# Two cross-attentions over 77 keys on one Trainium2 core: dense queries with masked keys, row sums taken with the values, division in token order

## The reference, cut to what matters

```python
    def _L0_xattn_ref(x, y, q_w, q_b, kv_w, kv_b, qn_w, qn_b, kn_w, kn_b, out_w, out_b):
        q = (x @ q_w.T + q_b).reshape(b, s1, H, hd).transpose(0, 2, 1, 3)
        kv = (y @ kv_w.T + kv_b).reshape(b, s2, 2, H, hd).transpose(2, 0, 3, 1, 4)
        k, v = (kv[0], kv[1])
        q = _layernorm(q, qn_w, qn_b)
        k = _layernorm(k, kn_w, kn_b)
        q = _apply_rope(q) * scale
        attn = jnp.einsum('bhqd,bhkd->bhqk', q, k)
        attn = jax.nn.softmax(attn, axis=-1)
        o = jnp.einsum('bhqk,bhkd->bhqd', attn, v)
        o = o.transpose(0, 2, 1, 3).reshape(b, s1, c)
        return o @ out_w.T + out_b
    def _L1_xattn_ref(xq, xkv, Wq, Wkv, Wout, bout):
        q = (xq @ Wq.T).reshape(B, SQ, NUM_HEADS, HEAD_DIM)
        kv = (xkv @ Wkv.T).reshape(B, SKV, 2, NUM_HEADS, HEAD_DIM)
        k, v = (kv[:, :, 0], kv[:, :, 1])
        att = jax.nn.softmax(jnp.einsum('bxhd,byhd->bhxy', q, k) * scale, axis=-1)
        x = jnp.einsum('bhxy,byhd->bxhd', att, v).reshape(B, SQ, H)
        return x @ Wout.T + bout
```

## Time and profile before

| | |
|---|---|
| runs | 2087.87, 2095.12, 2100.6 us; median 2095.12 |
| the profiled execution | 2091.41 us; span 2089.7 us from its first to its last instruction |
| mean granted TensorE clock | 0.933 |
| busy share of the span | PE 86%, PEld 68%, DVE 56%, ACT 48%, POOL 36% |
| L0x | about 330 to 568 us of the span; its loop 367 to 552 |
| L1x | about 1337 to 1534 us; its loop 1366 to 1520 |

### The profile page before, as it was taken

One profiled execution on the slowest core, in us unless ns is written; L12 is line 12 of the kernel. 1 busy time (PEld: TensorE's weight loads), 2 busy tenths in 40 slices (PEclk: granted clock), 3 DMA queues, 4 the chain that ended last, 5 costly groups with the idle time before them and its releaser, 6 DMA issues. The chain is left out here.

```text
span 2089.7 us, 41893 instructions
## 1 busy us (share of the span) xinstructions
PE 1797.7 (86%) x15668; PEld 1421.4 (68%) x15668; DVE 1178.4 (56%) x3027; ACT 1003.5 (48%) x2376; POOL 745.4 (36%) x680
## 2 busy tenths in 40 slices
PE   6889875899659999769999999599959995999994
PEld 5767764676448888646777776476647774788883
DVE  3666664575454545435555555456548782457774
ACT  4655552354234545345554445244436662356663
POOL 2434342776314242323333333311124452334443
PEclk9999998998779999979999999799969997999997
DMA  2000002000054342530000000201010415723334
GB/s 67 12 12 22 12 12 74 1 22 22 26 211 129 114 142 61 147 113 2 11 12 12 11 12 6 71 2 32 16 54 17 134 37 173 262 84 54 52 52 101
DMA packets 97872, 125.52 MB, mean 60 GB/s; under 512 B 8555, under 2 KB 84795, under 8 KB 97643
## 3 DMA queue, kind: packets, MB, share of 16 engines
q1 hardware_dynamic: 84378, 105.07, 15.3%
q0 software_dynamic: 13296, 17.77, 4.9%
HBM read 85.02 MB, written 39.89 MB: 60 GB/s over the span
## 5 line engine op out<-in xcount | busy, mean ns | idle before, releaser
L1876 POOL TENSOR_TENSOR L1a_probs<-L1a_probs,L1a_rinv 128x1024 f32<-128x1024 f32 x64 | 121.2, 1894 | 270.0 <-DVE L1a_rinv L2191 270.0
L1873 POOL TENSOR_TENSOR L0a_probs<-L0a_probs,L0a_rinv 128x256 f32<-128x256 f32 (+1 forms) x128 | 103.1, 826 | 189.6 <-DVE L0a_rinv L2191 189.6
L2183 DVE CUSTOM_DVE_ANT_0 L1a_sbias<-L1a_psS,L1a_bias 128x256 f32<-128x256 f32 x256 | 93.3, 421 | 108.7 <-PE L1a_psS L1984 108.6
L2136 ACT ACTIVATE L1a_probs<-L1a_sbias,L1a_nmx 128x256 f32<-128x256 f32 x256 | 126.5, 497 | 47.5 <-DVE L1a_nmx L2183 47.4
L2863 POOL DMA_INDIRECT moe_sums<-moe_y,moe_xg x39 | 83.4, 2139 | 134.3 <-DVE moe_y L3162 122.4
L2136 ACT ACTIVATE L0a_probs<-L0a_sbias,L0a_nmx 128x128 f32<-128x128 f32 (+1 forms) x256 | 112.8, 443 | 28.8 <-DVE L0a_nmx L2183 28.8
L2447 POOL DMA_INDIRECT ec_sums<-ec_yk,ec_token_at x32 | 59.0, 1845 | 189.1 <-ACT ec_yk L2568 184.2
L2633 DVE TENSOR_TENSOR ec_h<-ec_sg,ec_psU 128x512 f32<-128x512 f32 x64 | 44.0, 687 | 118.7 <-ACT ec_sg L2555 118.7
L2941 PE MATMUL moe_psY<-moe_wts,moe_hT 128*128 (+1 forms) x440 | 104.0, 379 | 0.8 <-ACT moe_hT L3008 0.8
L2183 DVE CUSTOM_DVE_ANT_0 L0a_sbias<-L0a_psS,L0a_later 128x128 f32<-128x128 f32 (+1 forms) x256 | 76.2, 354 | 44.3 <-PE L0a_psS L1981 43.9
L2480 PE MATMUL ec_psG<-ec_xs,ec_wt 128*128 128x512 f32 x384 | 99.0, 394 | 2.1 <-issue 2.1
(11 more groups left out here) (533 smaller groups left out, 5061.8 us busy)
## 6 DMA issues: line engine op xcount, KB each, us to landing
shelf<-in_L_ffn_w_gate SPq DMA_DIRECT2D x8, 1024.0 KB, 9.1
shelf<-in_L_ffn_w_up SPq DMA_DIRECT2D x8, 1024.0 KB, 12.8
ec_wd<-in_L_ffn_w_down SPq DMA_DIRECT2D x8, 1024.0 KB, 6.1
moe_rows<-blank SPq DMA_DIRECT2D x1, 5070.0 KB, 19.1
moe_xg<-moe_rows SPq DMA_DIRECT2D x39, 130.0 KB, 2.1
moe_wts<-in_L_ffn_e_gate SPq DMA_DIRECT2D x8, 512.0 KB, 10.2
moe_wts<-in_L_ffn_e_up SPq DMA_DIRECT2D x8, 512.0 KB, 9.9
moe_wts<-in_L_ffn_e_down SPq DMA_DIRECT2D x8, 512.0 KB, 10.1
```

Of the source, the lines that this page charges most:

```text
L1873: last = pool.tensor_tensor(v, v, bcast(rinv[:, r, :, t], 2, KEYS[t]), ALU.mult)
L1876: last = pool.tensor_tensor(v, v, bcast(rinv[:, r, :, :].rearrange("p h t -> p (h t)"), 2, S), ALU.mult)
L2136: ins = act.activation(probs[:, r, j, at], sbias[:, g % 2, j, at], ACT.Exp, bias=nmx[:, r, j, t:t + 1], scale=-1.0, accum_out=sums[:, r, j ...
L2183: last = dve.tensor_tensor_reduce(out=sbias[:, g % 2, j, at], in0=psS[:, slot + j, at], in1=added, scale=-1.0, scalar=LARGE, op0=ALU.add, ...
```

## The change

It is confined to `context_stage`, so to L0x and L1x.

- **Dense queries, masked keys.** Queries are kept as two tiles of 128 rows a batch with eight heads each, without padding. Keys come in two copies, `keys[:, o, par]`, multiplied by the mask `keep`, so that of two neighbouring heads one is zero. A second copy `marked`, made by GpSimd in `mark_keys`, has a one in a row that the masked head leaves free. `shift` no longer adds in place: it writes `shifted`, queries times `others` plus the transposed maxima. The turned scores multiply `marked` by `shifted`.
- **Row sums with the values.** The two unused 16-column groups of `vs` are 1 instead of 0, so that one product gives values and row sums. `row_sums` and `ones` are gone. `values` of the two steps go to the two halves of `psO`.
- **Division in token order.** ACT copies `psO` (`copy_values`), TensorE transposes it (`turn_values`), DVE's `out_norm` takes reciprocals of 8 columns and multiplies into `oM`, TensorE transposes back (`turn_back`), ACT rounds from `psO`, and `out_low` is now on DVE.
- **Order.** The transposed maxima have a bank of their own (`psT`, `turn_top`), and `NF` is 2. `turn_top` stands behind the second turned block instead of ahead of it. On DVE `row_max(n+2, 0)` stands ahead of `shift(n+1)`, and `spread` behind it.
- **Fronts.** Weight preparation is one operation for a matrix instead of four or eight, the masks are made on DVE (`set_masks`, `set_columns`) instead of memsets on GpSimd, and two broadcast transfers replace eight small ones. The `keep_busy` matmuls of the loops are gone; three (L0x) or six (L1x) stand in the fronts, beside the six ahead of L0x's first query item.

The core of the diff:

```diff
-    NF = 3
+    NF = 2
...
             def row_max(n, pair):
                 dve.wait_ge(s_ready[pair], n + 1)
                 if n >= 2:
-                    dve.wait_ge(item_ready, ready(("top",), n - 2))
+                    dve.wait_ge(top_ready, n - 1)
...
             def shift(n):
                 b, st = divmod(n, NST)
-                dve.wait_ge(item_ready, ready(("top",), n))
-                q = qs[:, b % 2, st, :]
-                dve.tensor_tensor(q, bank(("top",), n)[:, 0:S], q, ALU.add).then_inc(q_shifted, 1)
+                dve.wait_ge(top_ready, n + 1)
+                if n >= 2:
+                    dve.wait_ge(k_ready, 2 * n - 2)
+                dve.scalar_tensor_tensor(out=shifted[:, n % 2, :], in0=qs[:, b % 2, st // 2, :],
+                                         scalar=others[:, st % 2:st % 2 + 1], in1=psT[:, 0:S],
+                                         op0=ALU.mult, op1=ALU.add).then_inc(q_shifted, 1)
...
             def out_norm(o):
-                dve.wait_ge(r_ready, 2 * o + 2)
-                dve.reciprocal(rinv[:, o % 2, :], psO[:, S:2 * S]).then_inc(r_inverse, 1)
-                dve.wait_ge(r_inverse, o + 1)
-                if o >= 2:
-                    dve.wait_ge(o_low, o - 1)
-                dve.tensor_tensor(oN[:, o % 2, :], psO[:, 0:S], rinv[:, o % 2, :], ALU.mult).then_inc(o_norm, 1)
+
+                dve.wait_ge(o_turned, o + 1)
+                if o:
+                    dve.wait_ge(o_back, o)
+                turned = [psO[:, r * S:(r + 1) * S].rearrange("p (t j e) -> p (t j) e", t=TT, j=4) for r in range(2)]
+                for r in range(2):
+                    dve.reciprocal(rinv[:, r, :], turned[r][:, :, HD * (1 - r)]).then_inc(r_inverse, 1)
+                dve.wait_ge(r_inverse, 2 * o + 2)
+                for r in range(2):
+                    last = dve.tensor_tensor(oM[:, :, r, :], turned[r][:, :, HD * r:HD * (r + 1)], bcast(rinv[:, r, :], 2, HD),
+                                             ALU.mult)
+                last.then_inc(o_norm, 1)
...
+            def mark_keys(what, b):
+
+                wait_taken(pool, what, b)
+                o, at = key_columns(what, b)
+                for par in range(2):
+                    last = pool.tensor_scalar(marked[:, o, par, at], keys[:, o, par, at], one[:, par:par + 1], None, ALU.add)
+                last.then_inc(k_marked, 1)
...
+            def turn_top(n):
+
+                pe.wait_ge(s_max[0], n + 1)
+                pe.wait_ge(s_max[1], n + 1)
+                for t in range(TT):
+                    last = pe.transpose(psT[:, t * P:(t + 1) * P], top[:, n % 2, t, :], ident[:])
+                last.then_inc(top_ready, 1)
+
+            def turn_values(o):
+
+                pe.wait_ge(o_copied, o + 1)
+                for r in range(2):
+                    for t in range(TT):
+                        at = slice(r * S + t * P, r * S + (t + 1) * P)
+                        last = pe.transpose(psO[:, at], oE[:, at], ident[:])
+                last.then_inc(o_turned, 1)
+
+            def turn_back(o):
+
+                pe.wait_ge(o_norm, o + 1)
+                for t in range(TT):
+                    last = pe.transpose(psO[:, S + t * P:S + (t + 1) * P],
+                                        oM[:, 4 * t:4 * t + 4, :, :].rearrange("p j r d -> p (j r d)"), ident[:])
+                last.then_inc(o_back, 1)
...
             for n in range(N):
-                st = n % NST
                 turned_beside_scores(n, 0)
                 for what, b in slot(n, 0):
                     item(what, b)
                 if n:
                     values(n - 1)
-                if n + 1 < N:
-                    item(("top",), n + 1, (1, 0, 2, 0)[st] if rope else (1, 1 if n >= 4 * NST else 0, 0, 0)[st])
+                if n % 2 == 1 and n >= 3:
+                    turn_back((n - 3) // 2)
                 turned_beside_scores(n, 1)
-                if n:
-                    row_sums(n - 1)
+                if n + 1 < N:
+                    turn_top(n + 1)
+                if n % 2 == 0 and n >= 2:
+                    turn_values(n // 2 - 1)
                 for what, b in slot(n, 1):
                     item(what, b)
...
+            def copy_values(o):
+
+                act.wait_ge(v_done, 2 * o + 2)
+                if o:
+                    act.wait_ge(o_turned, o)
+                act.activation(oE[:], psO[:], ACT.Copy).then_inc(o_copied, 1)
...
                 b, st = divmod(n, NST)
                 if n + 1 < N:
                     row_max(n + 1, 1)
-                if st == 0 and b >= 2:
-                    spread(b - 2)
                 if rope and n == 2:
                     scale_k(1)
                 for what, at in slot(n, 0):
                     take(what, at)
+                if n + 2 < N:
+                    row_max(n + 2, 0)
                 if n + 1 < N:
                     shift(n + 1)
-                if n + 2 < N:
-                    row_max(n + 2, 0)
-                if st % 2 == 0 and n >= 2:
+                if st == 0 and b >= 2:
+                    spread(b - 2)
+                if n % 2 == 0 and n >= 2:
                     out_norm(n // 2 - 1)
+                if n % 2 == 1 and n >= 3:
+                    out_low((n - 3) // 2)
```

More of the change, by code:

```diff
@@ L426, in _ @@
                 b, st = divmod(n, NST)
-                if st % 2 == 1 and n >= 3:
-                    out_low(n // 2 - 1)
                 if st == 0 and b >= 2:
@@ L434, in _ @@
                     place_q(pool, 1)
+                for what, at in slot(n - 1, 1) + slot(n, 0) if n else []:
+                    if what[0] == "kT":
+                        mark_keys(what, at)
                 if rope and b + 2 < B:
@@ L560, in item @@
                                              start=(c == 0), stop=(c == KD - 1))
-                elif what[0] == "top":
-                    pe.wait_ge(s_max[0], b + 1)
-                    pe.wait_ge(s_max[1], b + 1)
-                    for t in range(TT):
-                        last = pe.transpose(ps[:, t * P:(t + 1) * P], top[:, b % 2, t, :], ident[:])
                 else:
@@ L665, in _ @@
             values(N - 1)
-            row_sums(N - 1)
+            turn_values(N // 2 - 1)
+            turn_back(N // 2 - 1)
             item(("out", 0), B - 1)
@@ L1064, in _ @@
             out_norm(N // 2 - 1)
+            out_low(N // 2 - 1)
             set_off(B - 2)
```

319 lines of the change are left out of this document (158 added, 161 removed).

## The result

Over 20 runs the changed kernel took 2080.97 us in the median (2068.48 to 2086.93), the kernel before 2100.7 (2087.23 to 2108.95, also 20 runs). The ratio is 0.9904, with a 95% interval of 0.9888 to 0.9920: 1.0% or about 20 us faster. The change measured is −20, and the median 2080.97 lies within rival A's 2060 to 2084, 6 us above the forecast because the kernel before was slower in these runs too.

What follows compares the result with a forecast made beforehand. TensorE was taken to bound the kernel; saved work, waits, fronts and clock summed to −12 us in L1x and −6 in L0x, from a profiled 2091.4 to 2073, stated as 2075 us for the median. The range was 2042 to 2107.

Steps and rivals of the forecast that it cites:

- rival A: Whole kernel: half the saved work is given back in waits, 2060 to 2084 us; chance 0.42.
- The bound: Both loops: TensorE is the bound, so work taken from it counts; net work L0x −23.1, L1x −27.6 us.
- The new waits: Both loops: waits that the new order brings, +16 us in L1x and +14 in L0x.
- the shift: End of steps: TensorE waits for the longer chain of maxima and shift, +10 us in L1x, +4 in L0x.
- The shorter reciprocals: Both loops: small reciprocals replace long ones and remove waits of the values, −5 us in L1x, −4 in L0x.
- the spread: Step 0 of a batch: LayerNorm statistics ahead of out_norm delay the next values, +6 us in L1x, +4 in L0x.
- ScalarE, +3: L0x's loop: ScalarE finishes a normalised row in front of an exponential in six batches, +3 us.
- GpSimd's marks: L0x: mark_keys on GpSimd stands ahead of the inverse roots, +3 us, bounds 0 and 13.
- The fronts: Before the loops: weight preparation saves about 2 us in L1x, masks, columns and first marks add 2 in L0x; together 0.
- a sign of being wrong: Fronts of both stages: the prediction is wrong if they move by over 5 us.
- The clock: Both loops: one or two further stretches at 1.2 GHz, +5 us in L0x, +7 in L1x; bounds −10 and +60.
- rival C: TensorE falls to 1.2 GHz in whole batches, clock under 0.85 in either loop, about 2117 us; chance 0.20.

Runs made afterwards that it cites:

- e8: The whole change with four dead matmuls of the row sums' size put back per step; 2116.57 us, ratio 1.0064 to the kernel before.
- e7: The whole change with shift(n+1) ahead of row_max(n+2, 0) on VectorE, as before; 2100.72 us, ratio 0.9998 to the kernel before.
- e9: The whole change with turn_top ahead of the second turned block and the shift ahead of row_max(n+2, 0); 2100.61 us, ratio 0.9883 to the kernel before.
- e3: The whole change with ScalarE instead of GpSimd making the marked keys in both stages; 2106.94 us, ratio 0.9918 to the kernel before.
- e1: The change in L1x only, L0x as in the kernel before; 2111.83 us, ratio 0.9929 to the kernel before.
- e10: The whole change with e9's order, e11's L0x edits and e6's places for the projections; ratio 0.9859 to the kernel before.
- e4: The whole change with the loops' keep-busy matmuls put back (24 in L0x, 12 in L1x); 2113.05 us, ratio 0.9937 to the kernel before.
- e6: The whole change with L1x's two output projections moved to the second halves of steps 2 and 3; 2078.37 us, ratio 0.9902 to the kernel before.
- e11: The whole change, in L0x only with ScalarE marking keys and masks and columns moved in the front; 2102.82 us, ratio 0.9910 to the kernel before.
- e12: The whole change with e9's order and e11's L0x edits, projections in the first halves; 2070.05 us, ratio 0.9857 to the kernel before.
- e2: The change in L0x only, L1x as in the kernel before; 2120.02 us, ratio 0.9970 to the kernel before.
- e5: The kernel before with only the two loops' keep-busy matmuls taken out; 2095.25 us, ratio 0.9993 to the kernel before.

## Why the prediction was right, step by step

- **The bound.** TensorE was the bound, and work taken from it did count: between the first and the last turned block L1x's TensorE time fell by 26.8 us (27.6 forecast; 29.1 in the earlier trace rows's stretches, 2.5 us of which lie outside the loop). L0x's fell by 16.2, where 23.1 of work less 5 for the clock were forecast. e8 gives back 18.6 us for 18.2 of row sums, 15.5 of them as work at the full clock; that it came so close is the clock's doing. The items that left are seen in the lines by form of L1x after the change, 84 instructions of query items instead of 168, and beside them the two new kinds of transposes:

```profile
L464 PE MATMUL L1x_psF<-L1x_xT,L1x_wqk 128*128 128x256 f32 x84 | 13.3, 294 | 0.2 <-issue 0.2
...
L580 PE MATMUL L1x_psO<-ident,L1x_oE 128*128 128x128 f32 x60 | 9.5, 282 | 0.0
...
L587 PE MATMUL L1x_psO<-ident,L1x_oM 128*128 128x128 f32 x30 | 6.8, 310 | 0.0
```

- **The new waits.** TensorE's idle time was forecast at 16 us in L1x and is 18.2, on the shift for 11.9 where 10 was said; at 20 in L0x, and it is 21.4. For the shift the mechanism was right and the size 20% low, with 0.36 us from the shift's end to TensorE, not 0.1. The reason that the prediction gave first, that `row_max(n+2, 0)` now comes ahead of the shift, was wrong: e7 shows that this order is no cost, and e9 that the place of the transposition on TensorE is what makes the wait. Two other terms hardly exist. The shorter reciprocals were credited with 5 us in L1x and the spread charged with 6, both at the values' wait of step 1; the exponential ends there within 0.16 us of the product in three of the four waits before, and within 0.08 after, and their total went from 4.1 to 3.4 us. In L0x no wait of the values on the product shows (spread, +4), and the waits on the exponential are 0.3 us (ScalarE, +3).
- **GpSimd's marks.** +3 was taken, between 0 and 13. They are 1.83 us a pair, as the row of L1s had it, and cost two waits of 2.9 and 2.7 us in the loop and some 1.7 us in the front. e3 removes them, though its time does not show it. The term was half of what it should have been, and no row of before could have shown that the keys' root would be late by so little more.
- **The fronts.** "Together 0" came out in the pair of traces, in two errors. Each front moved by more than the 5 us that the prediction had named as a sign of being wrong. L1x's was 6.1 us shorter and not 2: the front had held the key and query items of all four steps, and four of its eight items are gone, 3.1 us (1361.45 to 1364.54 in the trace of before) that the sum over the loop left out, while six keep-busy matmuls came in. Half of the 6.1 is the clock. The changed front took 29.3 to 30.0 us in five traces (the change, e1, e8, e9, e10), at a mean clock of 0.71 or 0.72, and 32.6 to 32.9 in five others (e4, e6, e7, e11, e12), at 0.63 or 0.64. That of before took 35.5 and 35.3 (e2) at 0.61 and 32.8 (e5) at 0.69. Like with like, the change saves some 3 us. L0x's front was 6.7 longer and not 2: masks and columns 1.8 us ahead of the key root, marks 1.7, and 3.2 us that no run takes apart, at a mean clock of 0.73 and not 0.77.
- **The clock.** +7 in L1x did not come: the clock is 0.96, and time lost to it in the loop 5.6 us (6.5 before). In both kernels nearly all of it lies in the last batch, where step 2 took 6.36 us before and 6.20 after, at 0.50. +5 in L0x was 10 in this pair of traces, (1 − 0.85) × 178 = 27 against 17, and 3 in the other (e1's 23 and e2's 26); rival C was to begin under 0.85, and this is at its edge. e4 shows that the keep-busy matmuls would not have prevented it there, e5 that they were worth little before. By the rule that transposes don't count as busy in the same way for the clock gate (the Trainium skill, "TensorE: Matmul & The Clock Gate", Part 4), L1x would have slowed too. It has 90 more of them in its loop and keeps its clock, 0.96. Whether they count in part, no run here shows.
- **By stage.** −12 and −6 were forecast; one stage at a time the runs give −15 and −6, within 9 to 22 and 1 to 12. L1x's loop was forecast at −9.6 and is 13.4 us shorter: the clock term of 7 did not come, and the waits' excess of 2.5 took part of that back. Its front gave 3 and not 2. L0x's loop was forecast at −8 and is 4.7 us shorter in the one pair of traces and 8.6 in the other (e1 against e2); its front is 5 to 7 us longer and not 2.

So the step that carried the forecast was right: TensorE is the bound, and a good part of the saved work comes back as waits, in L1x on the shift. That the total came so close is partly luck. In L1x the clock term that did not come was met in part by larger waits and by a little less work leaving. In L0x the spread's and ScalarE's 7 us, which did not come, were met by marks at twice their size and a longer front.

What was not settled: what sets L0x's clock, and how much of its front's length is the change's. No run changed these alone.

## What to carry to other kernels

When a step leaves the engine that bounds the kernel, look first at what it covered: list the chains between two of its blocks (here maxima, shift and exponential), and put the producer of the longest as early as its inputs allow. Moving other work between the halves mostly changes which chain is waited for: e6 took away 9 of 12 us of waits on the shift, and the loop became 2.7 shorter. Count the items of the fronts as well as those of the loops, and don't read a split by stage from one pair of profiles: the same stage differed by 7 us between two. At the full clock, by contrast, a batch of the changed L1x without a v item took 16.84 to 16.87 us in the traces of the change, e1 and e11. So compare steps at the full clock first, and the clock by itself.

## What the runs showed that was not expected

- With the keep-busy matmuls back (e4), L1x's clock is 1.00 and L0x's stays at 0.86. In L1x 6.4 us of dead work cost nothing in that trace, because the last batch kept the full clock.
- The time from the end of the operation that is waited for to the start of the waiting matmul differs by operation: 0.36 us behind VectorE's shift (1453.98 to 1454.34), 0.21 behind the maxima (e7), 0.15 behind ScalarE's exponential (e9).
- Two neighbouring operations on VectorE that are both needed by the same block do not commute in time: with the order changed a batch of L1x was 0.75 us longer, though the same two operations stood between the same two blocks.
